# Pairwise products of fields: operands of the product swapped, slots filled in either direction, 64 stores instead of 67

## What is computed

```python
# r_x: (4096, 32, 64) float32, L0_rec_W: (64, 64) float32
vid = jnp.einsum('bfd,de->bfe', x, W)
idx_i, idx_j = jnp.triu_indices(32, k=1)       # 496 pairs i < j
return x[:, idx_i, :] * vid[:, idx_j, :]       # (4096, 496, 64)
```

## Time and profile before

| | |
|---|---|
| median of 3 executions | 1284.48 us (1284.34 to 1284.66) |
| span of the profiled execution, first to last instruction | 1283.0 us |
| the median less this span | 1.5 us |
| DVE busy in the span | 1079.3 us (84%), 282 instructions |
| PE busy | 178.1 us (14%) |
| bytes moved by DMA | 553.73 MB: 33.62 MB read from HBM, 520.09 MB written |
| stores | 67 |

### The profile page before, as it was taken

One profiled execution on the slowest core, in us unless ns is written; L12 is line 12 of the kernel. 1 busy time (PEld: TensorE's weight loads), 2 busy tenths in 40 slices (PEclk: granted clock), 3 DMA queues, 4 the chain that ended last, 5 costly groups with the idle time before them and its releaser, 6 DMA issues. The chain is left out here.

```text
span 1283.0 us, 1129 instructions
## 1 busy us (share of the span) xinstructions
PE 178.1 (14%) x256; PEld 69.6 (5%) x256; DVE 1079.3 (84%) x282; POOL 0.2 (0%) x4
## 2 busy tenths in 40 slices
PE   3011030111120022011110301002103030111000
PEld 1000010000000010000000100001001010000000
DVE  6899988899999546898988999638988999999970
POOL 0000000000000000000000000000000000000000
PEclk8555565666555556565555656556656565665555
DMA  9999999999999999999999999999999999999999
GB/s 415 433 429 441 425 438 437 431 427 441 432 434 421 443 411 450 427 436 421 450 421 437 429 450 413 441 425 437 429 441 425 425 454 432 422 425 443 425 439 409
DMA packets 10946, 553.73 MB, mean 432 GB/s; under 512 B 1216, under 2 KB 1216, under 8 KB 1216
## 3 DMA queue, kind: packets, MB, share of 16 engines
q1 hardware_dynamic: 9936, 524.82, 94.7%
q10 hardware_dynamic: 1008, 28.90, 5.3%
HBM read 33.62 MB, written 520.09 MB: 432 GB/s over the span
## 5 line engine op out<-in xcount | busy, mean ns | idle before, releaser
L174 DVE TENSOR_TENSOR mem<-mem,vid 128x1024 f32<-128x1024 f32 (+11 forms) x282 | 1079.3, 3901 | 164.7 <-DMA out_dram<-mem 136.4
L236 PE MATMUL vid<-mem 128*128 (+1 forms) x256 | 178.1, 861 | 1003.6 <-PEq L235 1003.6
L236 PEld LDWEIGHTS vid<-mem 128*128 128x128 f32 x256 | 69.6, 286 | 1111.2 <-issue 1111.2
L338 POOL MEMSET const-bfloat16-1.0<- 128x1 bf16 x1 | 0.1, 101 | 0.0
L338 POOL MEMSET const-uint8-127<- 128x1 uint8 x1 | 0.1, 101 | 0.0
L338 POOL MEMSET const-float32-0.0<- 128x1 f32 x1 | 0.1, 98 | 0.2 <-issue 0.2
L338 POOL MEMSET const-float32-1.0<- 128x1 f32 x1 | 0.1, 98 | 0.0
## 6 DMA issues: line engine op xcount, KB each, us to landing
out_dram<-mem SPq DMA_DIRECT2D x11, 7680.0 KB, 22.6
out_dram<-mem SPq DMA_DIRECT2D x10, 7168.0 KB, 21.1
out_dram<-mem SPq DMA_DIRECT2D x5, 6656.0 KB, 20.6
out_dram<-mem SPq DMA_DIRECT2D x3, 6144.0 KB, 20.0
out_dram<-mem ACTq DMA_DIRECT2D x1, 7680.0 KB, 38.9
out_dram<-mem SPq DMA_DIRECT2D x1, 5120.0 KB, 19.5
out_dram<-mem SPq DMA_DIRECT2D x1, 4608.0 KB, 20.9
out_dram<-mem SPq DMA_DIRECT2D x1, 4096.0 KB, 20.6
```

Of the source, the lines that this page charges most:

```text
L174: self.engine.tensor_tensor(*operands, MULT).then_inc(self.dve, 1)
L236: nc.tensor.matmul(vid[:, b * BANK : b * BANK + BANK, :], lhsT=w, rhs=mem[:, bass.ds(k * step + (first + b * BANK), BANK), :], start=True, ...
L338: nc = _bacc.Bacc("TRN2", target_bir_lowering=False, num_devices=1, dynamic_dma_scratch_size=256)
```

## The change

Three things are changed together.

1. **The product.** x of one field is repeated, and vid of n neighbouring fields is read in a row; before it was the other way round. The blocks of a tile are cut and ordered anew: `by_block(up)` has fourteen blocks with at most 8 x 16 products (before thirteen, one of them 16 x 16). In tiles with `up` the host stores x with its fields reversed, and the field on the left of a pair is the larger index of the stored order, so that the pair is still (smaller, larger) of the true fields. In tiles 6 to 10, which walk downward in `mem`, the indices are mirrored. `banks(up)` says which half of vid is made first.
2. **The slots.** A negative size marks a slot that is filled from its upper end down. SLOTS has 64 entries, 43 of them with 128 units; before it had 67, 34 of them with 128. CUTS has more entries and often two cuts in a slot. The program has 379 products on DVE instead of 282. Bytes and matmuls are the same.
3. **The hold behind a load.** SP now holds the next store until the stretch's first load has landed, not until PE's first matmul. The loads stand behind 22 and 42 slots.

```diff
-WALKS = [(range(1), 0, 32), (range(1, 6), 286, 32), (range(6, 11), 128, -32), (range(11, 16), 286, 32)]
+WALKS = [
+    (range(1), 0, 32, True),
+    (range(1, 6), 286, 32, True),
+    (range(6, 11), 128, -32, False),
+    (range(11, 16), 286, 32, True),
+]
...
 SLOTS = [
-    (120, 32), (128, 158), (104, 32), (80, 136), (64, 222), (120, 32), (128, 158), (128, 16),
...
+    (112, 32), (128, 144), (112, 32), (-112, 174), (-120, 54), (104, 174), (112, 24), (128,
...
 CUTS = {
-    3: (22,), 5: (104,), 6: (64,), 7: (16,), 8: (14,), 10: (16,), 28: (32,), 31: (56,),
...
+    3: (14,), 4: (30,), 6: (30,), 7: (38,), 8: (23,), 9: (24,), 10: (31,), 11: (30, 30), 12:
...
-LOAD_BEHIND = [24, 45]
+LOAD_BEHIND = [22, 42]
...
+    def blocks():
+        yield from within(0)
+        yield row(8, 0, 8, 8)
+        yield row(16, 0, 16, 8)
+        yield from within(16)
+        yield row(24, 0, 16, 8)
+        yield row(24, 16, 8, 8)
+
+    for rows, n, v, dv, x, dx in blocks():
+        if not up:
+            v = F - 1 - (v + (rows - 1) * dv + n - 1)
+            x = F - 1 - (x + (rows - 1) * dx)
+        yield rows, n, v, dv, x, dx
...
+def spot(slot, pos, n):
+    size, _ = SLOTS[slot]
+    off = pos - STARTS[slot]
+    return off if size > 0 else -size - off - n
...
             if m == 1:
-                left = xt[:, i : i + n, :]
-                right = vid[:, j : j + 1, :].to_broadcast([P, n, C])
+                left = xt[:, i : i + 1, :].to_broadcast([P, n, C])
+                right = vid[:, j : j + n, :]
             else:
                 o = o.rearrange("p (m w) c -> p m w c", m=m)
-                right = vid[:, j : j + (m - 1) * dj + 1 : dj, :].unsqueeze(2).to_broadcast([P, m, n, C])
-                if di == 0:
-                    left = xt[:, i : i + n, :].unsqueeze(1).to_broadcast([P, m, n, C])
+                left = xt[:, i : i + (m - 1) * di + 1 : di, :].unsqueeze(2).to_broadcast([P, m, n, C])
+                if dj == 0:
+                    right = vid[:, j : j + n, :].unsqueeze(1).to_broadcast([P, m, n, C])
...
-                    stretch(sp, tiles, runs, f"g{slot}_")
-                    held = pe, tiles[0] * (F // BANK) + 1
+                    held = stretch(sp, tiles, runs, f"g{slot}_")[-2], 16
```

More of the change, by code:

```diff
@@ L21 @@
 UNITS = 446
-WALKS = [(range(1), 0, 32), (range(1, 6), 286, 32), (range(6, 11), 128, -32), (range(11, 16), 286, 32)]
-PLACE = [first + step * k for tiles, first, step in WALKS for k in range(len(tiles))]
+WALKS = [
[4 more added lines that the diff above has]
+]
+PLACE = [first + step * k for tiles, first, step, _ in WALKS for k in range(len(tiles))]
+UP = [up for tiles, _, _, up in WALKS for _ in tiles]
 HEAD = range(6), [(16, 16), (286, 128), (414, 16), (430, 16)]
@@ L60, with by_block, step, row @@
 PAD0 = 8
-STARTS = [0, *accumulate(n for n, _ in SLOTS)]
-def by_block():
+STARTS = [0, *accumulate(abs(n) for n, _ in SLOTS)]
+def by_block(up):
+    def step(lo, b, c, d):
+        return 16 // b, c, lo, b, lo + c + d, b
+    def row(x, v, n, rows):
+        return rows, n, v, 0, x, 1
     def within(lo):
-        yield "step", lo, 2, 1, 0
+        yield step(lo, 2, 1, 0)
         for k in range(2):
-            yield "step", lo, 4, 2, k
+            yield step(lo, 4, 2, k)
         for i in (lo, lo + 8):
[L72 to L87, removed]
+            yield row(i + 4, i, 4, 4)
+    def blocks():
[10 more added lines that the diff above has]
+        yield rows, n, v, dv, x, dx
+def products(t, ends):
+    at = t * NP
+    for rows, n, v, dv, x, dx in by_block(UP[t]):
         r = k = 0
@@ L94, in products @@
                 m, w = min(rows - r, room // n), n
-            yield at, m, w, i0 + r * di + k, di, j0 + r * dj, dj
+            yield at, m, w, x + r * dx, dx, v + r * dv + k, dv
             at += m * w
@@ L100, in products, with banks @@
                 k += w
+def spot(slot, pos, n):
+    size, _ = SLOTS[slot]
+    off = pos - STARTS[slot]
+    return off if size > 0 else -size - off - n
+ENDS = sorted({*STARTS, *(STARTS[k] + c for k, cuts in CUTS.items() for c in cuts)})
 HALF = F // 2
+def banks(up):
+    half = list(range(HALF // BANK))
+    return half + [b + HALF // BANK for b in half] if up else [b + HALF // BANK for b in half] + half
 def fields(tiles, lo, n):
@@ L226, in build @@
     held = stretch(act, *HEAD, "h")[-2], 16
-    for tiles, first, step in WALKS:
+    for tiles, first, step, up in WALKS:
         with nc.tensor.Fori(0, len(tiles)) as k:
-            for b in range(F // BANK):
-                if b % (HALF // BANK) == 0:
+            for i, b in enumerate(banks(up)):
+                if i % (HALF // BANK) == 0:
                     nc.tensor.wait_ge(go, 1)
@@ L242, in build @@
                 ).then_inc(pe, 1)
-    ends = sorted({*STARTS, *(STARTS[k] + c for k, cuts in CUTS.items() for c in cuts)})
     vector = Products(nc.vector, dve)
@@ L254, in build @@
     for t in range(NT):
-        place = PLACE[t]
-        for b in range(0, F // BANK, HALF // BANK):
-            for s in [ws, *(loaded[t, f] for f in range(b * BANK, b * BANK + HALF))]:
+        place, order = PLACE[t], banks(UP[t])
+        for h in range(0, F // BANK, HALF // BANK):
+            half = order[h : h + HALF // BANK]
+            for s in [ws, *(loaded[t, b * BANK + f] for b in half for f in range(BANK))]:
                 act.after(s)
-            act.after_products(max(bank_read[b : b + HALF // BANK]))
+            act.after_products(max(bank_read[b] for b in half))
             nc.scalar.sem_inc(go, 1)
@@ L263, in build @@
         start = done
-        for pos, m, n, i, di, j, dj in products(t * NP, ends):
+        for pos, m, n, i, di, j, dj in products(t, ENDS):
             begin = STARTS[slot]
-            size, lo = SLOTS[slot]
-            u = lo + pos - begin
+            size, lo = abs(SLOTS[slot][0]), SLOTS[slot][1]
+            u = lo + spot(slot, pos, m * n)
             o = mem[:, u : u + m * n, :]
             if m == 1:
-                left = xt[:, i : i + n, :]
-                right = vid[:, j : j + 1, :].to_broadcast([P, n, C])
+                left = xt[:, i : i + 1, :].to_broadcast([P, n, C])
+                right = vid[:, j : j + n, :]
             else:
                 o = o.rearrange("p (m w) c -> p m w c", m=m)
-                right = vid[:, j : j + (m - 1) * dj + 1 : dj, :].unsqueeze(2).to_broadcast([P, m, n, C])
-                if di == 0:
-                    left = xt[:, i : i + n, :].unsqueeze(1).to_broadcast([P, m, n, C])
+                left = xt[:, i : i + (m - 1) * di + 1 : di, :].unsqueeze(2).to_broadcast([P, m, n, C])
+                if dj == 0:
+                    right = vid[:, j : j + n, :].unsqueeze(1).to_broadcast([P, m, n, C])
                 else:
-                    left = xt.rearrange("p (m d) c -> p m d c", d=di)[:, i // di : i // di + m, i % di : i % di + n, :]
+                    right = vid.rearrange("p (m d) c -> p m d c", d=dj)[:, j // dj : j // dj + m, j % dj : j % dj + n, :]
             waits = {}
-            need = t * (F // BANK) + (j + (m - 1) * dj) // BANK + 1
+            used = range(j // BANK, (j + (m - 1) * dj + n - 1) // BANK + 1)
+            landed = {f // HALF * (HALF // BANK) for f in (i, i + (m - 1) * di)}
+            need = t * (F // BANK) + max(order.index(b) for b in {*used, *landed}) + 1
             if need > dve_pe:
@@ L292, in build @@
             for r in range(m):
-                for f in range(i + r * di, i + r * di + n):
-                    track.read[place + f] = done
-                bank_read[(j + r * dj) // BANK] = done
+                track.read[place + i + r * di] = done
+            for b in used:
+                bank_read[b] = done
             if pos + m * n == begin + size:
@@ L323, in build, with positions @@
     nc.sync.sem_inc(final, -16)
-def pairs():
-    for _, m, n, i, di, j, dj in products(0, [NP]):
+def positions(t):
+    for pos, m, n, i, di, j, dj in products(t, ENDS):
+        slot = bisect_right(STARTS, pos) - 1
+        at = STARTS[slot] + spot(slot, pos, m * n)
         for r in range(m):
             for k in range(n):
-                yield i + r * di + k, j + r * dj
+                p = i + r * di, j + r * dj + k
+                yield tuple(F - 1 - f for f in p) if UP[t] else p, at + r * n + k
 _INS = ["r_x", "L0_rec_W"]
@@ L342 @@
     x = x.reshape(2, NT, C, F, D).transpose(0, 4, 1, 3, 2).reshape(P, NT, F, C)
+    x = _np.stack([x[:, t, ::-1] if UP[t] else x[:, t] for t in range(NT)], 1)
     w2 = _np.zeros((P, P), _np.float32)
@@ L358 @@
     r = _run(nc, [arrays], core_ids=[0])
-    got = r.results[0]["out_0_dram"][:, : NT * NP].reshape(2, D, NT, NP, C)
+    got = r.results[0]["out_0_dram"][:, : NT * NP].reshape(2, D, NT * NP, C)
     place = {p: k for k, p in enumerate((i, j) for i in range(F) for j in range(i + 1, F))}
     res = _np.empty((2, NT, C, NP, D), _np.float32)
-    order = [place[p] for p in pairs()]
     for t in range(NT):
```

(5 more changed lines are left out.)

## The result

| | before | changed |
|---|---|---|
| median of 19 executions each | 1284.53 us | 1286.49 us |
| lowest and highest | 1284.22 to 1285.10 | 1285.97 to 1287.14 |
| ratio | | 1.0015, 95% interval 1.0009 to 1.0022 |
| span of the profiled execution | 1283.0 us | 1285.2 us |

The changed kernel is 2.0 us slower. That is less than the 2.6 us that I took as the limit of "no change", but it is clear of zero, it has the other sign than the forecast of 1284.2, and it lies above the range of 1283.2 to 1285.8.

A forecast was written before the change was run, and what follows sets the result against it. DMA engines bound the kernel from end to end. Span 1283.0 us less 0.3 for three fewer stores gives 1282.7; with 1.5 us around it, 1284.2 us. Range: 1283.2 to 1285.8 us.

The forecast's parts named there:

- DMA is the bound, the changed slots feed it, and no more than 2.4 us can be won: Whole stream: transfers take 1250.5 of the 1252.9 us left after the first store's issue; gaps together about 2.4 us.
- The leads at slots 31 and 45: Time from a store's issue to the landing of the transfer ahead: 3.3 us at both; 2.4 left no gap.
- One sign of the list: Expected in the changed profile: two 128-unit stores landing 38.7 us apart even around slots 31 and 45.
- The swapped product costs nothing, 97 products more cost 7 us of DVE and no time: DVE products: 0% dearer per element; 97 more add 7.8 us to DVE's 1079.3, no time while leads hold.
- The rival in which DVE becomes the bound: DVE products with vid in a row dearer: 1285.5 us at 10%, 1293 at 15%; 7% chance in all.
- the late refill: Rival at tile boundaries: vid's refill takes over 8.7 us and stalls DVE; 1286.4 us at 2 us late; 3% chance.
- Three stores fewer, 0.3 us: Store queue: 27 packets fewer on each engine at 0.012 us each save 0.3 us, with 0 as the other end.
- The rival in which each store costs a latency: Between stores: engines pause 2.4 us each, so three fewer give 7.2 us, 1277.3 us; 2% chance.
- The weighing of the Trainium skill: Stores: the page's fit, about 2.0 us plus bytes over 436 GB/s, gives 6 us less; rejected for landings 19.35 us apart.
- The hold behind loads: Stores s22 and s42 behind the load stretches: issued when the first load lands, lead 4.8 us instead of 2.4.
- a bubble of 0.9 us: Each load stretch: 44.4 us for units that take 43.5, kept unchanged; rival of losing it, 1.8 us less, 3% chance.

The follow-up runs named there:

- lead24: Changed kernel with each stretch's 32-unit second load cut into 16 and 16, so the hold ends 2.4 us before the last landing: 1284.74 us, 1.0000; again 1285.10 us, 1.0003.

## Why the prediction was wrong

- **DMA is the bound, the changed slots feed it, and no more than 2.4 us can be won:** right. The leads at slots 31 and 45 came out at 3.2 to 3.3 us where 3.3 was forecast. No experiment got more than 0.1 us below the kernel before. One sign of the list was a little off: two stores around slot 45 land 39.4 us apart instead of 38.7 (935.55 to 974.99). They do so in lead24 as well (933.29 to 972.72), so it isn't part of the loss.
- **The swapped product costs nothing, 97 products more cost 7 us of DVE and no time:** right, 8681 ns and 1215 ns as before (the form of 16384 elements, which the prediction names as well, doesn't occur in the changed kernel), and lead24 keeps them all at ratio 1.0000. The rival in which DVE becomes the bound falls, and the late refill too: DVE waits for PE three times, as before.
- **Three stores fewer, 0.3 us:** not shown. lead24 came out 0.03 and 0.43 us above the kernel before, with two loads more in it. The term is too small to be seen. The rival in which each store costs a latency, which gave 1277.3, falls with it.
- **The weighing of the Trainium skill** ("DMA: Bandwidth & Descriptors", section "Anatomy of one DMA — SWDGE (gpsimd) path"): the row was right to prefer. The page gives its fit for DMAs that GpSimd issues; nearly all stores here are issued by SP. An estimate by that fit for lead24, with three stores fewer and two loads more, is 2 us under the kernel before; it was 0.03 and 0.43 us above.
- **The hold behind loads:** this is the step that failed. The prediction found the leads right, "4.8 where it was 2.4", and took a longer lead for a safer one. It asked only what a short lead costs. A store 4.8 us ahead of the end of a load costs 1.4 us at the first stretch and 1.7 at the second, by the landings. Put back to 2.4 us, in lead24, it gives the time back; moved to 4.8 us in the kernel before, it costs 1.2 us. The ledger: 3.1 us lost at the landings of the loads, 2.2 us in the span. The landings are those of the slowest engine. On average over the engines the load packets are 1.9 us longer (1.0 and 0.8). The engines' last packets end 1.3 us later than before on average; one engine ends 1.6 us behind the other fifteen, where before it was 0.4, and the kernel ends with it. Some of the difference may be the packets saved, and the switch into the loads varies by some tenths from one profile to the next.
- **The rivals:** none of them was this one. The one that ended on the slow side put the danger on DVE. Rows 2 showed a rate per share that never moved, and I took a packet's time as fixed. But the rows of the two load stretches were the place to look: a bubble of 0.9 us stood there, and I noted it as a constant that the change can't touch. The change had its one real wait edit right beside it. The old hold until PE's first matmul looks like a detour, and its effect was to time the store to 2.4 us before the end of the load.
- **The range:** it had no bound for this term. Pricing it by the nearest row, the bubble of 0.9 us a switch, would have given 1.8 us more for the case, 1286.0. That takes the range nearer to the result of 1286.49, but not up to it.

## What to carry to other kernels

In a stream that is bound by DMA, the end of a load is an event of its own: look at what is issued behind its last packets, and try a few moments for the first store. Here 2.4 us before the load's last landing was best, and neither 4.8 nor 1.2 was as good. When an edit replaces what a wait waits for, work out the new moment of issue and ask what it does in both directions, earlier and later. Read the rate beside the share: a share of 0.96 at 229 GB/s is engines that are slow, not full. And look at every place where a thing happens: in two of the runs the second load stretch went otherwise than the first, and each changed what could be concluded.

## What was not expected of the hardware

- With a store issued 4.8 us or more before the end of a load, the load's packets are slow for 2 to 3 us near its end: from 410 to 442 GB/s down to 164 to 311 in one-us windows, at a share from 0.63 to 1.3. The dose, as time of the kernel before plus, each with an interval of about 1.2 us to either side: at a lead of 1.2 us 1.5 us (0.9 of it idle engines, no slow packet), at 2.4 us 0.0 to 0.4, at 3.6 us 0.8, at 4.8 us 1.7 to 2.0 in the changed kernel and 1.2 in the kernel before, and at 14 to 22 us (no hold) 1.5.
- It isn't bound to a store: behind a load issued at 873.1, with no store queued, the rate fell to 213 GB/s at a share of 1.10, though that cost no time (1284.84 us).
- A store's first packets start 0.84 to 1.0 us after its issue when the engines are free (877.92 to 878.07 for an issue at 877.08).
- It doesn't depend on DVE: the rate fell with DVE idle (393, 229, 164 GB/s in the kernel before with the new hold) as with DVE busy.
- The loss isn't regained. Once the loads are late, the stream behind runs at its 433 to 434 GB/s with nothing to spare, and 3.1 us at two switches come out as 2.2 us at the end of 1285.

Why the load's packets become slow, whether it is what the engine has to do for the transfer that is queued next or something else in it, no run here shows. The slow stretches of the changed kernel, of the one without a hold and of the load behind a load all begin 1.0 to 1.5 us after the landing of the 128-unit load; lead24 has such a landing too and no slow packet, so that landing alone doesn't explain them.
